# Indirect row transfers in pairs over four slots, and an order written out for nine opening and four closing slots

## The reference

```python
x = L0_attn_x                                  # (4, 1024, 128)
xn = layernorm(x)                              # no weights
s = xn
for i in range(6):                             # attention stack
    h = layernorm(s) * ln1_w[i] + ln1_b[i]
    q, k, v = h @ wq[i], h @ wk[i], h @ wv[i]  # 8 heads of 16
    q = softmax(q, over the 16 of a head);  k = softmax(k, over the 1024 tokens)
    s = (q @ (k^T v)) @ wo[i] + bo[i] + s
    h = layernorm(s) * ln2_w[i] + ln2_b[i]
    s = leaky_relu(h @ w1[i], 0.01) @ w2[i] + s        # 128 -> 512 -> 128
probs = softmax(xn @ router_w^T + router_b)            # 8 experts
y = (xn @ expert_w[top1]^T + expert_b[top1]) * max(probs)
out = x + s * silu(y)
```

## Time and profile before

| | us |
|---|---|
| median of three runs | 647.32 |
| the three runs | 644.05, 647.82, 647.32 |
| the profiled execution, as timed | 641.02 |
| its span, first to last instruction | 639.3 |
| PE busy in it | 595.2 |
| DVE busy in it | 529.4 |

### The profile page before, as it was taken

The page is one execution under the profiler, slowest core; times in us unless marked ns, Lnnn a source line. Parts: engine busy times, 40 slices in busy tenths (PEclk is TensorE's granted clock), DMA queues, the critical chain, the costliest instruction groups (busy, mean ns, idle before and its releaser), DMA issues.

```text
span 639.3 us, 12643 instructions
## 1 busy us (share of the span) xinstructions
PE 595.2 (93%) x4206; PEld 531.7 (83%) x4206; DVE 529.4 (83%) x1342; ACT 442.1 (69%) x773; POOL 309.5 (48%) x308
## 2 busy tenths in 40 slices
PE   7897899999899899999999999999999989899984
PEld 6886788887688789999898898898897887798874
DVE  5667388989979699889889989989989879888755
ACT  2447447767577588788788688778777768678640
POOL 7743422327776733423324434324427687755253
PEclk9789699999899899999999999999999999999996
DMA  8920012133241443443354353453333262331011
GB/s 258 392 76 2 0 67 99 35 132 115 64 146 63 154 137 93 141 165 119 113 165 133 110 188 103 126 170 117 99 133 118 60 176 81 97 132 68 1 66 67
DMA packets 59107, 73.20 MB, mean 115 GB/s; under 512 B 6306, under 2 KB 49314, under 8 KB 59043
## 3 DMA queue, kind: packets, MB, share of 16 engines
q1 hardware_dynamic: 56560, 68.18, 32.4%
q0 software_dynamic: 2048, 4.20, 2.3%
q10 hardware_dynamic: 434, 0.02, 0.0%
HBM read 39.87 MB, written 32.51 MB: 113 GB/s over the span
## 4 chain that ended last, share of the span: by engine, by line
PE 67%; DVE 15%; POOL 10%; issue 6%; DMA 1%; ACT 1%; SPq 0%; DVEq 0%; POOLq 0%; ACTq 0%
PE psY L495 18%; PE psT L574 6%; PE psH L384 6%; PE psT L379 6%; PE psH L385 5%; PE psH L386 5%; PE psS L540 5%; PE psM L520 4%; PE psT L508 4%; DVE st L895 3%; POOL sorted_x L1452 3%; POOL qsm L1506 2%; POOL gate L1460 2%; POOL rstd L1415 2%; DVE X L1157 2%
## 5 line engine op out<-in xcount | busy, mean ns | idle before, releaser
L495 PE MATMUL psY<-w_all,hid 128*128 128x128 f32 x1536 | 191.6, 277 | 4.0 <-DVE hid L1147 2.0
L495 PEld LDWEIGHTS psY<-w_all,hid 128*128 128x128 f32 x1536 | 184.4, 194 | 7.2 <-issue 2.4
L1147 DVE TENSOR_TENSOR hid<-psH,hsl 128x512 f32<-128x512 f32 x192 | 122.8, 675 | 47.0 <-ACT hsl L713 45.6
L713 ACT ACTIVATE hsl<-psH 128x512 f32<-128x512 f32 x192 | 111.0, 594 | 51.0 <-PE psH L386 48.1
L1415 POOL TENSOR_TENSOR rstd<-veps,minus_half 128x8 f32<-128x8 f32 x44 | 72.3, 1642 | 91.7 <-DVE veps L912 91.7
L1484 POOL TENSOR_TENSOR xn_lo<-xn,xn_hi 128x512 fp32r<-128x512 f32 x48 | 61.1, 1275 | 94.0 <-ACT xn_hi L777 94.0
L384 PE MATMUL psH<-xn_hi,w_hi 128*128 128x512 f32 x192 | 87.8, 457 | 15.6 <-POOL xn_lo L1484 9.7
L1506 POOL TENSOR_TENSOR qsm<-qe,qrec 128x1024 f32<-128x1024 f32 x24 | 46.5, 1939 | 77.9 <-DVE qrec L1230 77.8
L743 ACT ACTIVATE xh<-X,shift,rstd 128x128 f32<-128x128 f32 x188 | 77.0, 483 | 5.0 <-POOL shift L1418 4.9
L386 PE MATMUL psH<-xn_lo,w_hi 128*128 128x512 f32 x192 | 77.6, 404 | 0.0
L385 PE MATMUL psH<-xn_hi,w_lo 128*128 128x512 f32 x192 | 77.5, 404 | 0.0
(11 more groups left out here) (163 smaller groups left out, 1064.5 us busy)
## 6 DMA issues: line engine op xcount, KB each, us to landing
through<-turn SPq DMA_DIRECT2D x22, 512.0 KB, 2.8
turn<-through SPq DMA_DIRECT2D x88, 128.0 KB, 2.8
through<-blocks SPq DMA_DIRECT2D x20, 512.0 KB, 3.3
turned<-through SPq DMA_DIRECT2D x80, 128.0 KB
wb<-expert_rows SPq DMA_DIRECT2D x40, 128.0 KB, 2.1
sorted_x<-blocks SPq DMA_DIRECT2D x5, 512.0 KB, 6.1
xs_xsT<-sorted_x SPq DMA_DIRECT2D x10, 256.0 KB, 3.0
sorted_y<-ys SPq DMA_DIRECT2D x10, 256.0 KB, 2.4
```

Of the source, the lines that this page charges most:

```text
L495: last = nc.tensor.matmul(tile(psY, t), tile(hid[:, c, :], t), w2_all[:, n // NBATCH, c, :], start=(c == 0 and t == 0), stop=(c == NC - 1) ...
L713: nc.scalar.activation(hsl[:, i % 2, :], psH[:, i % 2, :], ACT.Copy, scale=SLOPE) \
L1147: nc.vector.tensor_tensor(hid[:, i % NC, :], psH[:, i % 2, :], hsl[:, i % 2, :], ALU.max) \
```

## The change

Five things are changed.

1. `move_rows` takes a quarter: eight transfers a slot, in four pairs, scatter in slots 6 to 9, gather in slots 21 to 24. The experts' groups run one slot later (`FIRST` = 11).
2. `slot(s)` now runs only for s = 10 to 23. Its order is changed in a few places, shown below.
3. All that stood in slots 4 to 9 and in the prologue is written out step by step on every engine, with an order of its own on each; so are slots 24 to 27.
4. `normalise_input` is cut into two halves, and the set-up of constants and the loads stand in another order: `ident` before the head mask, the zeros for `sorted_x` late, layer 0 of `w1` second in SP's queue, the later layers of `w2` in the middle of the opening.
5. Nothing that computes on the data is added or removed.

The core of the diff; the written-out lists are cut to the stretches of which the prediction speaks.

```diff
@@ POOL @@
+            def move_rows(s, quarter):
+
+                if 6 <= s < 10:
+                    scatter(range(8 * (s - 6) + 2 * quarter, 8 * (s - 6) + 2 * quarter + 2))
+                if 21 <= s < 25:
+                    gather(range(8 * (s - 21) + 2 * quarter, 8 * (s - 21) + 2 * quarter + 2))
...
+            ranks()
+            identity()
+            heads()
+            half_negative()
+            first_deviations(0)
+            input_deviations(0)
+            normalise_input(0, 0)
+            first_deviations(1)
+            normalise_input(0, 1)
+            no_rows()
...
+            scale_queries(1)
+            input_deviations(3)
+            normalise_input(3, 0)
+            earlier_tokens()
+            split_w1(0)
+            normalise_input(3, 1)
+            deviations2(1)
+            low_part(0, 0)
+            low_part(0, 1)
+            scale_queries(2)
...
             def slot(s):
+                move_rows(s, 0)
+                move_rows(s, 1)
                 if s % NBATCH == 3 and s < ITEMS:
                     split_w1(s // NBATCH)
                 low_part(s - 3, 0)
+                low_part(s - 3, 1)
                 deviations2(s - 2)
-                low_part(s - 3, 1)
+                move_rows(s, 2)
+                move_rows(s, 3)
                 deviations1(s)
-                move_rows(s, 0, 5)
...
                 scale_queries(s - 1)
-                move_rows(s, 5, 11)
...
+            scale_queries(23)
+            low_part(22, 0)
+            low_part(22, 1)
+            deviations2(23)
+            move_rows(24, 2)
+            move_rows(24, 3)
+            low_part(23, 0)
+            weigh(3)
+            low_part(23, 1)
+            add_input(1, 2)
+            add_last_input()
             add_input(2, 4)
@@ PE @@
+            warm_up()
+            value_bias(0)
             first_items_by_feature(0)
...
+            attention(1)
             normalised_tiles(2, 1)
             norm2_by_feature(0)
             logits(2)
             first_items_by_feature(3)
             output_bias(2)
             normalised_tiles(3, 0)
+            key_sums(2)
             normalised_tiles(3, 1)
+            hidden(0, 0)
+            hidden(0, 1)
...
             def slot(s):
+                if group_of(s) is not None:
+                    turn_rows(group_of(s))
                 attention(s - 2)
                 output(s - 4, 4)
...
+                queries_by_feature(s - 1)
                 mixing(s - 1)
-                queries_by_feature(s - 1)
@@ DVE @@
             def slot(s):
                 add_y(s - 4, 0)
+                statistics1(s, 0)
                 ...
+                leaky(s - 4, 6)
+                leaky(s - 4, 7)
                 add_attention(s - 2)
...
+            gate_last()
+            gated(2)
+            leaky(23, 4)
+            leaky(23, 5)
+            last_output(0)
+            leaky(23, 6)
+            leaky(23, 7)
             last_output(1)
```

More of the change, by code:

```diff
@@ L281, in _ @@
[L281 to L286, removed]
@@ new lines, in _ @@
+            output(3, 0)
+            queries(5)
+            output(3, 1)
+            output(3, 2)
+            hidden(3, 4)
+            keys_by_token(5)
+            output_bias(5)
+            output(3, 3)
+            key_sums(5)
+            hidden(3, 5)
+            context(5)
+            queries_by_feature(5)
+            mixing(5)
+            hidden(3, 6)
+            hidden(3, 7)
+            attention(5)
+            output(3, 4)
+            keys(6)
+            queries(6)
+            output(3, 5)
@@ new lines, in _ @@
+            output(4, 5)
+            hidden(5, 0)
+            hidden(5, 1)
+            mixing(6)
+            output(4, 6)
+            output(4, 7)
+            hidden(5, 2)
+            attention(6)
+            hidden(5, 3)
+            output(5, 0)
+            output(5, 1)
+            keys(7)
+            hidden(5, 4)
+            queries(7)
+            keys_by_token(7)
+            output(5, 2)
+            output(5, 3)
+            hidden(5, 5)
+            key_sums(7)
+            hidden(5, 6)
@@ new lines, in _ @@
+            context(7)
+            queries_by_feature(7)
+            mixing(7)
+            hidden(5, 7)
+            attention(7)
+            queries(8)
+            keys(8)
+            output(5, 4)
+            output(5, 5)
+            output(5, 6)
+            output(5, 7)
+            hidden(6, 0)
+            hidden(6, 1)
+            keys_by_token(8)
+            output(6, 0)
+            hidden(6, 2)
+            hidden(6, 3)
+            key_sums(8)
+            output(6, 1)
+            output(6, 2)
@@ L659, in slot @@
[L659 to L660 removed]
+                hidden(s - 3, 2)
+                hidden(s - 3, 3)
                 keys_by_token(s - 1)
[L662 to L664 removed]
+                output(s - 3, 0)
+                output(s - 3, 1)
                 key_sums(s - 1)
@@ new lines, in _ @@
+            hidden(21, 1)
+            hidden(21, 2)
+            queries(23)
+            hidden(21, 3)
+            keys(23)
+            output(21, 0)
+            hidden(21, 4)
+            output(21, 1)
+            output(21, 2)
+            keys_by_token(23)
+            output(21, 3)
+            hidden(21, 5)
+            key_sums(23)
+            hidden(21, 6)
+            context(23)
+            queries_by_feature(23)
+            mixing(23)
+            hidden(21, 7)
+            attention(23)
```

1047 lines of the change are left out of this document (805 added, 242 removed).

## The result

The changed kernel takes 609.00 us (median of 4 runs, 606.65 to 609.72); the kernel before took 645.68 us beside it (4 runs, 643.02 to 647.82). The ratio is 0.943, 95% interval 0.938 to 0.948. The profiled executions have spans of 604.9 and 639.3 us, 34.4 us apart; the medians are 36.7 us apart. The forecast was 613 us, with a sum of 34.

What follows compares the result with a forecast made beforehand. PE was taken as the bound, with DVE second and near, and 59 us lost in loose stretches. Gains 13 + 10 - 1 + 5 + 7 = 34 off the 647.3 median gave 613 us; forecast range 604 to 619.

Steps and rivals of the forecast that it cites:

- The opening: Up to slot 4: 22 us lost to PE waits and low clock; 13 taken back, bounds 6 and 18.
- The walk: New opening lists timed with the trace's durations, each step after its engine and waits; 17 us ahead by ranks.
- Slots 4 to 9: 18 us lost; between 3 and 14 can return, 10 taken, near DVE at 95% busy.
- the second rival: DVE bounds slots 4 to 9, which give 3; the opening's head start gives 9 instead of 13; total 624 us; 22%.
- the forecast's price: Slots 4 to 9: six slots at 22.19 us plus some 1.9 for ranks and layer biases, 135 against 152.9 taken.
- The upper bound of 14: Slots 4 to 9: the most of the 18 us lost there that could come back.
- Slots 10 to 19: Steady slots, same work with small reorderings; 1 us lost taken, bounds -0.5 and +5.
- Slots 20 to 23: 8.5 us lost to PE's waits for scaled queries and low_part; 5 taken back, bounds 2 and 7.
- The transfers set it: Slots 20 to 23: the last transfer ended where the queries' scaling began, 517.31, so transfers set PE's wait.
- The close: From slot 24 on: 10.7 us lost; 7 taken back, bounds 3 and 10.
- PE stopped from 622.76 to 631.19, 8.4 us: The close: DVE stood in last_output(0), waiting for POOL's add_input (3.27), with the last two leaky steps behind it.
- The lock in every slot: Slots 10 to 23: paired low_parts hold DVE's small statistics operations 3.1 us each through shared ports; 656 us; 4%.

Runs made afterwards that it cites:

- the transfers alone: Kernel before with eight row transfers a slot in pairs over four slots, FIRST = 11 and GpSimd's changed slot order; ratio 0.990.
- the first experiment: Kernel before with stage_w1(0) on VectorE moved from behind add_attention(1) to behind statistics2(0); 631.8 us against 640.4, ratio 0.989.
- with pairs: Changed kernel with slot 6's row of six cut to four and, from slot 10 on, transfers in four separate pairs a slot; 604.6 us, ratio 0.944.
- the one with eleven transfers: Changed kernel with eleven, eleven and ten transfers in slots 6 to 8 and 21 to 23, in rows of six and five; 618.2 us, ratio 0.958.
- the 44 transposes: Kernel before with 44 unused identity transposes on PE filling its wait ahead of hidden(0, 0); ratio 0.999.
- the opening undone: Changed kernel with prologue and slots 4 to 9 in the order of before, eleven transfers in slots 6 to 8; 627.6 us, ratio 0.980.
- the bias late: Kernel before with the router bias broadcast issued behind ScalarE's input of item 0 instead of ahead of everything; ratio 1.000.
- slot 6's row cut: Changed kernel with one pair of slot 6's transfers moved behind item 3's two low parts, making the row of six four; 603.4 us, ratio 0.934.
- the last one: Changed kernel with slot 6's row of six cut to four, low_part(23, 1) ahead of weigh(3), last leaky steps ahead of last_output's addition; 598.9 us, ratio 0.9405.

## Why the prediction was right, and where it was off

*The opening: taken 13, bounds 6 and 18; measured 19.2, above the upper bound.* The walk was right (`key_sums(1)` at 38, was 36.09; `hidden(0, 0)` near 56, was 54.70; 17 ahead by `ranks`, was 19.2 at the point of equal work). What failed is the step after it, "A walk leaves out every small hand-over. I take 13 of the 17": no such loss appeared, because a walk with before's durations also leaves out a gain, the matmuls that got faster. 8.0 of the 19.2 us are that. The first transposes moved 1.1 us earlier, not 1 us later: the late bias closed a gap in the loads that I had not seen in the rows, and the warm-up, which would have taken the place of the loads as the wait, begins 0.8 us earlier.

*Slots 4 to 9: taken 10, measured 6.0.* The step at fault is the share of VectorE: it was busy 132.4 of 146.9 us, 90%, which is the figure of the second rival, not the 95% of the forecast. But VectorE's load alone did not set their time. Cutting one row of transfers brought 3 us more in this stretch, and the transfers alone gave 6.3 without the written-out order. So a part of what the forecast put down to VectorE is behind the row: 3.3 us of standstill, the clock at 0.89 after it. With these 3 us back the stretch would still take 144 us where the forecast's price was 135; no run shows what holds those 9. The upper bound of 14 had no row behind it, either: VectorE at 95% gives 10.6.

*Slots 10 to 19: taken 1 lost.* With the group that moved, 233.20 + 1.18 = 234.4 against 233.66: 0.7 lost. All of it is in slot 10, which took 23.1 us without a group where 22.2 were due; the nine behind it took 23.34 each, as short as before.

*Slots 20 to 23: taken 5.* 97.31 - (93.74 - 1.18) = 4.75. No wait for `qsm`, as said. Yet slots 22 and 23 took 24.2 and 23.5, over the 23.2 that I named. And the reason I gave is only half of it. "The transfers set it" was read from the scaling that starts where the last transfer ends; four transfers stand ahead of the scaling in one experiment, and nothing waits for it. Eight in rows of four instead of eleven in rows of five and six is what counts: with eleven at the changed places slots 21 to 23 cost 3.3 to 3.8 us more each.

*The close: taken 7, measured 5.1.* The step held: VectorE's 1.71 us of idle ahead of the addition, for `add_last_input`, is gone. But "PE stopped from 622.76 to 631.19, 8.4 us" misreads the chain. It is without a PE step there, not PE without work; the timeline of before has PE busy for 4.4 us of it, with two waits of 2.0 us, and the clock at 0.50 behind the second:

```profile
626.22 2.97 PE L495 MATMUL psY<-w_all,hid 128*128 128x128 f32 x16 [1.99 <-DVE gate L1134]
631.19 3.78 PE L495 MATMUL psY<-w_all,hid 128*128 128x128 f32 x16 [2.00 <-DVE hid L1147]
```

```profile
631.19:635.00 3.81, 3.78 (x16) 3.49 (x16) 0.55 (x1) 0.00 (x0) 0.00 (x0) 0.50 0.43 167
```

In the changed kernel the first of the waits is gone, the second is 1.09 us, and the same sixteen matmuls behind it take 2.05 us at a clock of 1.00. Two waits that I had priced at nothing and at 1 us were left, for `low_part(23, 1)` behind `weigh(3)` (1.0) and for `leaky(23, 6)` behind `last_output(0)` (1.09); taking them out gave 1.3. The chain of the changed kernel, starts and lengths, against the earlier trace rows:

```profile
594.39 0.69 DVE gate L1545
595.20 0.48 issue
595.69 2.13 issue
597.83 0.69 DVE hid L1558
598.56 2.07 PE psY L515 x16
```

The 2.13 are the addition of `last_output(0)`. The timeline of the two engines says what held it:

```profile
595.13 2.77 DVE L1549 TENSOR_TENSOR xraw<-xraw,gate 128x512 f32<-128x512 f32 x1
...
601.44 0.69 DVE L1549 TENSOR_TENSOR xraw<-xraw,gate 128x512 f32<-128x512 f32 x1
...
594.98 2.38 POOL L2157 TENSOR_TENSOR xraw<-xraw,gate 128x1024 f32<-128x1024 f32 x1
```

The same addition takes 0.69 us alone and 2.77 beside GpSimd's addition, and ends 0.5 us behind it. In the earlier trace rows the 2.50 us of "issue" behind GpSimd's `xraw` stand at the same place, where I had read only the wait for the 3.27 ahead of them. The Trainium skill, "SBUF — State Buffer", section "Who interferes with whom", has a VectorE instruction with two SBUF inputs held by a GpSimd instruction that reads SBUF; by that rule, the trace agrees.

*The rivals.* The lock in every slot fell: the steady slots' `negmean` has a mean of 180 ns. That VectorE bounds the opening slots fell with the first experiment, though its 90% was right. So 19.2 + 6.0 - 0.7 + 4.8 + 5.1 = 34.4, against 13 + 10 - 1 + 5 + 7 = 34. That the sum is this close is luck: an opening that was 6 short and two terms that were 6 long in all made up for each other. The order of the terms, and that each stretch but the steady one gains, was not. (The chances given for "faster" add up to 0.93, not 0.92.)

## What to carry to other kernels

When a stall goes from a stretch where TensorE's clock is below 1, count the work behind it at the full clock as well; here that was 8 of 19 us. Spread indirect transfers from GpSimd so that no more than about four stand in a row, even where its list has room for them: what a long row holds up need not be on its list. Before crediting an edit with a wait that is gone, look whether a second execution of the same code has it. And in a walk over a list written by hand, look at what stands between an engine's two halves of one product (`low_part`, `leaky`): TensorE asks for both.

## What the runs showed that was not expected

*Rows of indirect transfers.* Behind rows of five to eight (0.95 us each, 0.30 between them) waits of VectorE and ScalarE for matmuls that had long ended lasted up to 4.1 us, and nearly all of them ended 0.3 to 1.4 us after the end of the row; two ended 0.1 us ahead of it, and two in the midst of the row of eight. Behind rows of four they lasted 0.9 to 1.8 us; with pairs there were none in slots 21 to 23. Without a named releaser they stand behind one row of the changed kernel and of each kernel that keeps its row of six, behind five rows of the one with eleven transfers, and behind rows of five and six of all four kernels above that have those of before: five rows with one step of the opening, seven with the 44 transposes, two with the opening undone, five with the bias late.

In the kernel before itself such rows stand in six slots, and none of its waits lacks a releaser in the trace. But that is one execution. The kernel with the bias late has the same lists but for one load, and its trace has the waits. The same step in slot 20, before and then there:

```profile
490.62 0.38 PE L548 MATMUL psS<-gT,wv_all 128*128 128x128 f32 x2
491.04 0.29 DVE L1245 TENSOR_TENSOR ctxT<-psS,head_mask 128x128 f32<-128x128 f32 x1 [0.45 <-PE psS L548]
```

```profile
489.19 0.38 PE L548 MATMUL psS<-gT,wv_all 128*128 128x128 f32 x2
491.93 0.29 DVE L1245 TENSOR_TENSOR ctxT<-psS,head_mask 128x128 f32<-128x128 f32 x1 [2.82 <-remote]
```

The row of five began 4.4 us ahead of the matmuls in both and ended 1.3 us behind them; VectorE saw them done after 0.04 us in one and after 2.36 in the other. So a row makes such waits possible and does not always bring them, and whether one comes seems to vary from one execution to the next, as with the rows of four in slots 21 to 23, which have such waits in the kernel with slot 6's row cut (1.0 to 1.4 us) and none in the last one. Each kernel has one trace here, so how often they come is not known. Through what a row delays a signal between two other engines stays open, too; no run tried it.

*The warm-up.* The same 64 transposes, begun at 2.60 us, ended at 11.38 in one execution and at 12.56 in another (and took 8.6 to 10.0 us in the traces with that start); in the second, they and not the loads were what the first real work waited for.
